# Attention block: probabilities normalised on POOL before the block transpose, instead of outputs divided after the product

## The reference

```
h    = group_norm(x) * gn_w + gn_b
q, k, v = qw h + qb,  kw h + kb,  vw h + vb
attn = softmax(q^T k / sqrt(128), axis=-1)        # 1024 x 1024
out  = v attn^T                                   # 128 x 1024
y    = x + pw out + pb
```

## Time and profile before

| | |
|---|---|
| median of 3 runs | 145.03 us |
| profiled execution | 144.35 us |
| its span, first to last instruction | 142.4 us |
| mean granted TensorE clock | 0.998 |
| busy: PE, DVE, ACT, POOL | 90%, 70%, 47%, 19% |

### The profile page before, as it was taken

One profiled execution on the slowest core, in us unless ns is written; L12 is line 12 of the kernel. 1 busy time (PEld: TensorE's weight loads), 2 busy tenths in 40 slices (PEclk: granted clock), 3 DMA queues, 4 the chain that ended last, 5 costly groups with the idle time before them and its releaser, 6 DMA issues.

```text
span 142.4 us, 1927 instructions
## 1 busy us (share of the span) xinstructions
PE 127.7 (90%) x628; PEld 108.4 (76%) x628; DVE 99.4 (70%) x171; ACT 66.5 (47%) x107; POOL 26.9 (19%) x33
## 2 busy tenths in 40 slices
PE   0399986874999999999999999999999999999990
PEld 0397864544888888888888888888888888888880
DVE  0566899999667978889887877977777855711122
ACT  4055457876145666454454674644533454330300
POOL 5056034510002026021002350030003000300300
PEclk9999999999999999999999999999999999999999
DMA  4950000089929950998099636893796659980031
GB/s 146 302 215 0 0 0 0 2 184 204 199 63 201 209 122 5 205 209 177 0 204 201 155 107 148 203 206 111 158 209 139 161 130 206 204 275 0 0 110 37
DMA packets 8041, 19.26 MB, mean 135 GB/s; under 512 B 2144, under 2 KB 2912, under 8 KB 8032
## 3 DMA queue, kind: packets, MB, share of 16 engines
q1 hardware_dynamic: 8032, 19.15, 55.9%
HBM read 2.36 MB, written 2.10 MB: 31 GB/s over the span
## 4 chain that ended last, share of the span: by engine, by line
PE 80%; DVE 6%; DMA 5%; SPq 4%; issue 2%; ACT 0%; DVEq 0%
PE ACC L273 34%; PE S L239 9%; PE S L240 8%; PE S L243 8%; DMA w_in<-weights 3%; PE A L223 3%; SPq L138 3%; PE A L289 2%; DVE blocks L516 2%; PE S L298 2%; PE ACC L298 2%; DVE s_sb L507 2%; DMA pT<-blocks 2%; PE A L257 2%; DVE bn L442 1%
## 5 line engine op out<-in xcount | busy, mean ns | idle before, releaser
L507 DVE TENSOR_SCALAR_CACHE_REDUCE s_sb<-S,row_term 128x1024 f32<-128x1024 f32 x32 | 40.9, 1278 | 19.9 <-PE S L243 19.9
L273 PE MATMUL ACC<-pT,v 128*128 128x256 f32 x224 | 53.0, 381 | 0.7 <-DMA pT<-blocks 0.7
L273 PEld LDWEIGHTS ACC<-pT,v 128*128 128x128 f32 x224 | 41.2, 190 | 6.1 <-ACT v L370 0.9
L378 ACT ACTIVATE s_sb<-s_sb,rowmin 128x1024 f32<-128x1024 f32 x32 | 36.8, 1151 | 18.7 <-DVE s_sb L507 18.7
L516 DVE STREAM_TRANSPOSE blocks<-s_sb 128x1024 f32<-128x1024 f32 x28 | 34.7, 1240 | 0.0
L239 PE MATMUL S<-h_hi,g_hi 128*128 128x512 f32 x64 | 30.4, 475 | 2.6 <-DVE s_sb L507 2.5
L240 PE MATMUL S<-h_lo,g_hi 128*128 128x512 f32 x64 | 25.1, 393 | 0.0
L243 PE MATMUL S<-h_hi,g_lo 128*128 128x512 f32 x64 | 19.9, 392 | 0.0
L638 POOL TENSOR_TENSOR xb<-rden_bc,xb 128x512 f32<-128x512 f32 x7 | 8.9, 1276 | 57.3 <-DVE rden_bc L529 57.3
L239 PEld LDWEIGHTS S<-h_hi,g_hi 128*128 128x128 f32 x64 | 12.1, 189 | 6.0 <-DVE s_sb L507 2.9
L370 ACT COPY v<-A 128x384 f32<-128x384 f32 (+1 forms) x12 | 5.3, 442 | 19.1 <-PE A L223 19.1
(11 more groups left out here) (80 smaller groups left out, 108.1 us busy)
## 6 DMA issues: line engine op xcount, KB each, us to landing
pT<-blocks SPq DMA_DIRECT2D x112, 128.0 KB, 2.4
out<-xb SPq DMA_DIRECT2D x7, 256.0 KB, 2.7
x_sb<-x SPq DMA_DIRECT2D x1, 1536.0 KB, 8.4
x_sb<-x SPq DMA_DIRECT2D x2, 256.0 KB, 2.9
w_in<-weights SPq DMA_DIRECT2D x1, 256.0 KB, 4.8
out<-xb SPq DMA_DIRECT2D x2, 128.0 KB, 1.9
cols<-vectors SPq DMA_DIRECT2D x1, 3.0 KB, 2.7
```

The source lines that it names most:

```text
L273: last = pe.matmul(to, v[:, b % 3, t, :], pT[:, g % 2, 2 * pair:2 * pair + 2, t, :], start=(t == 0), stop=(t == KT - 1))
L378: act.activation(s_sb[:, c % 3, :], s_sb[:, c % 3, :], ACT.Exp, bias=rowmin[:, c % CH:c % CH + 1], scale=-1.0, accum_out=den[:, g % 2, k:k ...
L507: dve.tensor_scalar(s_sb[:, c % 3, :], S[:, c % 2, :], row_term[:, b % 2, i:i + 1], None, ALU.add, ALU.min, accum_out=rowmin[:, i:i + 1]). ...
```

## The change

Each tile of probabilities is multiplied by the reciprocals of its own row sums, in place, before it is transposed. There the sums lie on the partitions like the rows. DVE takes the reciprocal of one column per step, POOL does the multiplication, and only then may DVE (or PE, for the last group) transpose. `den` and `rden` hold 8 columns, one for each step of a batch. The broadcast of reciprocals on PE, ACT's copies of it and the division are gone, and `rden_bc` and `xb` with them: DVE adds the output in PSUM, the bias and x in one instruction, in place in `x_sb`. The product is now written to PSUM in query order, in runs of 32 columns. The core of the diff:

```
             def value_part(m):
...
-                to = ACC[:, g % 2, UW * pair:UW * (pair + 1)].rearrange("p (a n) -> p a n", a=2)
+                to = ACC[:, g % 2, :].rearrange("p (c a q) -> p a c q", c=GC, a=NQ)[:, 2 * pair:2 * pair + 2]
...
             def transpose_probs(c):
-                pe.wait_ge(probs_ready, c + 1)
+                pe.wait_ge(normed_ready, c + 1)
...
-            broadcast_rden(NG - 2)
-            broadcast_rden(NG - 1)
...
             def transpose_blocks(c):
-                dve.wait_ge(probs_ready, c + 1)
+                dve.wait_ge(normed_ready, c + 1)
...
-            def divide(g):
+            def invert_denominator(c):
+                dve.wait_ge(probs_ready, c + 1)
+                dve.reciprocal(rden[:, c % CH:c % CH + 1], den[:, c % CH:c % CH + 1]).then_inc(rden_ready, 1)
+
+            def finish(g):
+                b, f = g // 2, g % 2
                 dve.wait_ge(part_done, GC * (g + 1))
-                dve.wait_ge(bc_ready, g + 1)
-                by_rden = rden_bc[:, g % 2, :].rearrange("p (c a q) -> p a c q", c=GC, a=NQ)
-                dve.tensor_tensor(by_rden, ACC[:, g % 2, :].rearrange("p (a c q) -> p a c q", a=NQ, c=GC), by_rden, ALU.mult)\
-                   .then_inc(normed_ready, 1)
+                xs = x_sb[:, b, BANK * f:BANK * (f + 1)]
+                dve.scalar_tensor_tensor(xs, ACC[:, g % 2, :], out_bias[:, :], xs, ALU.add, ALU.add).then_inc(out_ready, 1)
...
             def finish_pair(r):
-                dve.wait_ge(bc_ready, NG)
                 dve.wait_ge(pair_done, r + 1)
-                cs = slice(PN * r, PN * (r + 1))
-                xs = xb[:, L, BANK + PN * r:BANK + PN * (r + 1)]
-                dve.tensor_tensor(rden_bc[:, 1, cs], pair_out[r], rden_bc[:, 1, cs], ALU.mult).then_inc(pair_normed, 1)
-                dve.wait_ge(pair_normed, r + 1)
-                dve.tensor_tensor(xs, rden_bc[:, 1, cs], xs, ALU.add).then_inc(pair_out_ready, 1)
+                xs = x_sb[:, L, BANK + PN * r:BANK + PN * (r + 1)]
+                dve.scalar_tensor_tensor(xs, pair_out[r], out_bias[:, :], xs, ALU.add, ALU.add).then_inc(pair_out_ready, 1)
...
+                if c > 0:
+                    invert_denominator(c - 1)
                 if c > LAG + GC - 1 and (c - LAG) % GC == 0:
-                    divide((c - LAG) // GC - 1)
+                    finish((c - LAG) // GC - 1)
                 drain_scores(c)
                 if 0 < c <= DIRECT:
                     transpose_blocks(c - 1)
...
+            def normalize_probs(c):
+                pool.wait_ge(rden_ready, c + 1)
+                pool.tensor_scalar(s_sb[:, c % 3, :], s_sb[:, c % 3, :], rden[:, c % CH:c % CH + 1], 1.0, ALU.mult, ALU.mult)\
+                    .then_inc(normed_ready, 1)
...
                 if i == 4 and b < L:
                     split_h(b + 1)
-                if c > LAG + GC - 1 and (c - LAG) % GC == 0:
-                    add_residual((c - LAG) // GC - 1)
-            add_residual(MOVED_GROUPS - 1)
+                if c > 0:
+                    normalize_probs(c - 1)
+            normalize_probs(STEPS - 1)
```

More of the change, by code:

```diff
@@ L87, in build @@
         rowmin = sb("rowmin", [P, CH])
[L88 to L91, removed]
+        den = sb("den", [P, CH])
+        rden = sb("rden", [P, CH])
         pT = sb("pT", [P, 2, NQ, KT, CQ])
@@ L116, in build @@
         v_psum, v_ready, row_ready = map(sem, ("v_psum", "v_ready", "row_ready"))
-        xb_ready = sem("xb_ready")
         scores_psum, rowmin_ready, probs_ready, blocks_ready = map(sem, ("scores_psum", "rowmin_ready", "probs_ready", "blocks_ready"))
@@ L121, in build @@
         part_done = sem("part_done")
-        rden_ready, bc_psum, bc_ready = map(sem, ("rden_ready", "bc_psum", "bc_ready"))
-        normed_ready, out_ready, stored = map(sem, ("normed_ready", "out_ready", "stored"))
+        rden_ready, normed_ready = map(sem, ("rden_ready", "normed_ready"))
+        out_ready, stored = map(sem, ("out_ready", "stored"))
         tp_psum, pair_done = map(sem, ("tp_psum", "pair_done"))
         pair_ready = [sem(f"pair_ready{f}") for f in range(HALVES)]
-        pair_normed, pair_out_ready = map(sem, ("pair_normed", "pair_out_ready"))
+        pair_out_ready = sem("pair_out_ready")
         block = ctx.enter_context(nc.Block())
@@ L144, in store_group @@
                 b, f = g // 2, g % 2
-                sp.dma_start(out[b, :, BANK * f:BANK * (f + 1)], xb[:, b, BANK * f:BANK * (f + 1)]).then_inc(stored, 16)
+                sp.dma_start(out[b, :, BANK * f:BANK * (f + 1)], x_sb[:, b, BANK * f:BANK * (f + 1)]).then_inc(stored, 16)
             for f in range(HALVES):
@@ L161, in _ @@
                 cs = slice(BANK + PN * r, BANK + PN * (r + 1))
-                sp.dma_start(out[L, :, cs], xb[:, L, cs]).then_inc(stored, 16)
+                sp.dma_start(out[L, :, cs], x_sb[:, L, cs]).then_inc(stored, 16)
                 if r == 0:
@@ L170, in group_deviations @@
                 pe.wait_ge(chan_ready, b + 1)
-                if b > 1:
-                    pe.wait_ge(bc_ready, 2 * b - 3)
+                if b > 0:
+                    pe.wait_ge(gvar_ready, b)
                 pe.matmul(A0[:, 0:1], deviation[:, :], chan[:, 0:1], start=True, stop=True).then_inc(dmean_psum, 1)
@@ L244, in scores @@
                 last.then_inc(scores_psum, 1)
[L246 to L258, removed]
             def value_part(m):
@@ L265, in value_part @@
                     if g > 1:
-                        pe.wait_ge(normed_ready, g - 1)
+                        pe.wait_ge(out_ready, g - 1)
                 if half == 0:
@@ L269, in value_part @@
                         pe.wait_ge(moved[g % 2][a], MOVED * (g // 2 + 1))
-                to = ACC[:, g % 2, UW * pair:UW * (pair + 1)].rearrange("p (a n) -> p a n", a=2)
+                to = ACC[:, g % 2, :].rearrange("p (c a q) -> p a c q", c=GC, a=NQ)[:, 2 * pair:2 * pair + 2]
                 for w in range(PT):
                     t = PT * half + w
-                    last = pe.matmul(to, v[:, b % 3, t, :], pT[:, g % 2, 2 * pair:2 * pair + 2, t, :], start=(t == 0), stop=(t == KT - 1))
+                    last = pe.matmul(to, v[:, b % 3, t, :], pT[:, g % 2, 2 * pair:2 * pair + 2, t, :].rearrange("p a (c q) -> p a c q", c=GC), start=(t == 0), stop=(t == KT - 1))
                 last.then_inc(part_done, 1)
             def transpose_probs(c):
-                pe.wait_ge(probs_ready, c + 1)
+                pe.wait_ge(normed_ready, c + 1)
                 for f in range(HALVES):
@@ L283, in transpose_probs @@
                     if c == DIRECT and f == 1:
-                        pe.wait_ge(bc_ready, NG - 2)
+                        pe.wait_ge(gvar_ready, B)
                     if c > DIRECT:
@@ L294, in value_pair @@
                     pe.wait_ge(pair_ready[f], 2 * (r + 1))
-                pe.wait_ge(normed_ready, MOVED_GROUPS - 1)
+                pe.wait_ge(out_ready, MOVED_GROUPS - 1)
                 to = pair_out[r]
@@ L323, in _ @@
                     value_tiles(b, 2)
-                    if b > 0:
-                        broadcast_rden(2 * b - 1)
                 if i == 6 and b < L:
                     project_g(b + 1, 0)
-                    broadcast_rden(2 * b)
                 if i == 7 and b < L:
@@ L373, in exponentials @@
             def exponentials(c):
-                g, k = c // GC, c % GC
                 act.wait_ge(rowmin_ready, c + 1)
-                if g > 1 and k == 0:
-                    act.wait_ge(rden_ready, g - 1)
                 act.activation(s_sb[:, c % 3, :], s_sb[:, c % 3, :], ACT.Exp, bias=rowmin[:, c % CH:c % CH + 1], scale=-1.0,
[L379 to L385, removed]
+                               accum_out=den[:, c % CH:c % CH + 1]).then_inc(probs_ready, 1)
             def copy_pair(c):
@@ L414, in _ @@
                     normalize(b + 1)
[L415 to L421, removed]
                 if i == 6 and b < L:
@@ L429, in _ @@
             copy_pair(STEPS - 1)
-            copy_rden(NG - 2)
-            copy_rden(NG - 1)
         @block.vector
@@ L582, in _ @@
                     transpose_blocks(c - 1)
-                if c % GC == 0 and c > 0:
-                    invert_denominators(c // GC - 1)
                 if i == 0:
@@ L598, in _ @@
                     copy_pair(c - 1)
-            invert_denominators(NG - 1)
+            invert_denominator(STEPS - 1)
             copy_pair(STEPS - 1)
-            divide(MOVED_GROUPS - 1)
+            finish(MOVED_GROUPS - 1)
             finish_pair(0)
```

## The result

The changed kernel took 153.31 us, median of 4 runs (152.1 to 153.47), against 145.67 for 4 runs of the kernel before (144.5 to 146.37): 1.051 times as long, 95% interval 1.042 to 1.061. The forecast was 152.2, in a range from 147.9 to 157.2. The profiled execution took 153.37, its span 151.6.

The account below looks back on a forecast made before the run. DVE was taken to set the pace in the first batch, PE after 34.8 us. Lost 5.85 + 4.3 + 1.2 + 0.1, gained 3.95: net 7.5 on 144.35, plus half of 0.7, gives 152.2 us, range 147.9 to 157.2.

Parts of the forecast that it names:

- Bound and relief: PE's path: 32 broadcast transposes gone, 3.5 us, and one operation less per finish at the end, 0.45; gained 3.95 us.
- first rival: POOL's detour hides everywhere and only PE's relief remains: 140.75 us, faster; chance 0.06.
- The hidden multiplication: Ordinary steps: POOL's multiplication, 1.12 us, at most 1.50, hides while DVE drains, with 0.3 us to spare.
- Batch 0: Step 4: multiplication behind split_h makes transpose 3 5.4 us later, first product moves from 34.80 to 40.2; 5.85 us lost.
- Batches 1 and 2: Step 4: transpose 3.1 us late behind split_h, group sent late, PE waits 2.15 us for DMAs each; together 4.3 us lost.
- The last tiles: Direct PE transposes wait for POOL's multiplication: 1.2 us lost at step 28, 0.1 at step 30.
- The product: Output product written to PSUM in runs of 32 columns: no cost taken, 2 us kept for the range.
- The sum: Whole kernel: lost 11.45, gained 3.95, net 7.5 us, so 151.85 from the profiled 144.35, and 152.2 us forecast.
- third rival: PE's clock falls in batch 0 while PE rests, costing 3.2 us: 155.4 us; chance 0.17.

Follow-up runs that it names:

- e1_relief: Changed kernel without the multiplication and reciprocals, transposes waiting for the exponential alone; 142.17 us, ratio 0.977 to the kernel before.
- e2_swap: Changed kernel with only POOL's order in step 4 changed: multiplication of step 3's tile ahead of split_h; 146.10 us, ratio 1.005 to the kernel before.
- e6_all: Changed kernel with multiplication before split_h, split_h halved, output product ahead of direct transposes, 29 extra matmuls in batch 0's PE waits; 142.73 us, ratio 0.987.
- e5_halves: Changed kernel with split_h cut into two halves, behind the multiplications of steps 4 and 5; 145.56 us, ratio 1.004 to the kernel before.
- e4_warm: Changed kernel with 13 extra PE matmuls before the scores of step 7 and 10 before step 8's value tiles; 151.98 us, ratio 1.048.
- e7_before_warm: Kernel before with 15 extra matmuls of 512 columns in PE's waits of batch 0; 144.83 us, ratio 1.001 to the kernel before.

## Why the prediction was right, point by point

- **Bound and relief.** Right in the mechanism. e1_relief shows 3.6 us where 28 transposes and one operation make 3.5. The prediction had 3.95, with the four transposes of step 6, and set their 0.44 us against it in batch 0's loss (5.85 for a delay of 5.4), so the net does not suffer; its first rival, 140.75, was 0.44 too low by it.
- **The hidden multiplication.** It took 1.12 us, as L631 had. In ordinary steps transposes stand directly behind the drain. The 1.54 us, an estimate from the best case in the Trainium skill (GPSIMD Engine Reference, section Elementwise — side-by-side cycle accounting), is too much; the measurement decides. I had put its effect on the sum at 1.5 us, but by the range's own count, five multiplications in the three chains, 0.42 more each would be 2.1.
- **Batch 0.** Transpose 3 was to run from 31.9 to 33.1 and ran from 31.55 to 32.8; the first product was to start at 40.2 and started at 40.19. e2_swap moves the transpose back by exchanging two lines, so POOL's order is shown to be the cause of its delay. It is not all of the 5.4 us: with POOL's order changed and split_h in halves the first product still starts at 36.65 to 36.80 (e6_all, e5_halves), some 2 us late by the length of the chain, which the prediction's times also held. That 40.2 was met to the hundredth is partly luck: the value tiles ahead of the product took 1.63 us at the slow clock, not 0.91, and at full clock the product would have started some 0.3 us earlier, an estimate from e4_warm, where it starts at 40.43 but the first scores already 0.5 us later than here.
- **Batches 1 and 2.** DVE waited 2.89 and 2.90 us, as foreseen (3.1 late). PE was to wait 2.15 us for the DMAs. It waited 1.44 for g_lo and 0.31 for the DMAs in batch 2, and 1.44 for g_lo in batch 1. The prediction had g_lo end inside the wait for the DMAs; it was the larger part. In size the term held: with the slower start behind the waits the delays are 1.98 and 2.24 us, 4.2 together for the 4.3 of the sum. That the size came out through another last wait is in part luck.
- **The last tiles.** One wait of PE for POOL, 0.96 us, before the first direct transpose; with the slower start behind it step 30 begins 1.18 us later, for the 1.2 of the sum.
- **The product.** 1.73 us for 8 with the strided writes, as before, and the mean of all 224 matmuls in e4_warm, at clock 1.00, is 381 ns as in the kernel before. The rule of the Trainium skill (SBUF — State Buffer, section Door 1: The DMA port swizzle), that any non-contiguous access pattern to PSUM significantly slows matmuls, does not hold for runs of 32 columns here.
- **The sum.** 7.5 us were predicted with the clock at 1.00. By the steps of the trace after it is 5.4 for batch 0, 4.2 for batches 1 and 2, 1.2 and 0.3 for the last tiles, less 3.5: 7.6, and 1.65 for the slow clock make the 9.2 by which the span grew. Runs of e4_warm at that clock have a median of 151.92 us; runs of the kernel before at 0.998 and over, made beside them, have one of 144.48: 7.4 us.
- **The clock.** The third rival, to which I gave 0.17, came true: the level of 1.2 GHz from within PE's waits of batch 0 until 44 us. Its price, for which I took 3.2 us, was 1.65 us in the trace and 1.3 between the medians. Less the 0.35 us that the forecast had added for the median, it is nearly all of the 1.1 us by which 153.31 lies above 152.2, a forecast that took the clock to stay at 1.00. So the mechanism was right and the assumption on the clock was not; the forecast stayed close because the price was half of what I wrote. I had thought the pauses of the kernel before harmless; by e7_before_warm even they let the clock fall in 9 runs of 23. The profiled execution, on which the prediction went, was one in which it had not.

## What to carry to other kernels

When work moves to an idle engine, read that engine's list in order and ask, for each instruction ahead of the new one, what it waits for: POOL was busy 19% of the time, and one instruction that waited for a third engine made the new one 3 us late three times. Such a lateness reaches the engine that bounds by two ways: through a transfer that starts only when the last of a group is ready, and through all that stands behind the late instruction on its own engine, which here was the longer way in batches 1 and 2. Before a comparison of one or two per cent, list the granted clock of each run: the same program gave 144.4 and 146.3 us.

## What the runs showed of the hardware

- In the trace of the kernel after the granted clock fell to 0.50 at 33.5 us, while PE waited from 31.0 to 34.1, and was back at 1.00 at 43.7, PE having worked without a gap since 38.8. In e1_relief, whose longest wait before it was 2.1 us, it fell at 34.9, when PE had just gone back to work, until 38.3. Extra matmuls in the waits of batch 0 kept the mean at 0.998 or more in 21 of 22 runs (e4_warm, e6_all, e7_before_warm); the 15 of e7_before_warm cost 0.2 us.
- A POOL multiplication of 128x1024 by a column took 1.12 us, of 128x512 0.69; split_h with two inputs took 2.39 and 1.30.
- Products written to PSUM in 8 runs of 32 columns take 0.216 us each, as in one run of 256.
